# Weaving each layernorm's chunks into the residual loop that feeds it

## The reference, cut to what matters

```python
def _layernorm(x, eps=1e-5):
    m = jnp.mean(x, axis=-1, keepdims=True)
    v = jnp.var(x, axis=-1, keepdims=True)
    return (x - m) / jnp.sqrt(v + eps)

x = x + attn_a(_layernorm(x), ...)   # q, k, v; circular binding of k and v summed over
                                     # the tokens; unbinding of the sum with q
x = x + ffn(_layernorm(x), ...)      # 8 experts of rank 16, the best 2 by gate logits
x = x + attn_b(_layernorm(x), ...)   # layernorms its input again; 16 heads, sigmoid scores
x = x + ffn(_layernorm(x), ...)
```

## Time and profile before

| | us |
|---|---|
| runs of the kernel | 2741.25, 2744.46, 2745.48 (median 2744.46) |
| the profiled execution, its time | 2747.32 |
| its span on the slowest core (core 3) | 2745.8 |
| spans of the 8 cores | 2723.5 to 2745.8 |
| PE busy / DVE / ACT in the span | 1518.3 / 1105.6 / 678.2 |
| mean granted TensorE clock | 0.707 to 0.709 of full speed |

### The profile page before, as it was taken

One profiled execution on the slowest core, in us unless ns is written; L12 is line 12 of the kernel. 1 busy time (PEld: TensorE's weight loads), 2 busy tenths in 40 slices (PEclk: granted clock), 3 DMA queues, 4 the chain that ended last, 5 costly groups with the idle time before them and its releaser, 6 DMA issues.

```text
span 2745.8 us, 19739 instructions; the slowest of 8 cores (2723.5 to 2745.8 us)
## 1 busy us (share of the span) xinstructions
PE 1518.3 (55%) x5930; PEld 574.3 (21%) x5930; DVE 1105.6 (40%) x1281; ACT 678.2 (25%) x677; POOL 36.2 (1%) x58
## 2 busy tenths in 40 slices
PE   1699956131111535448223887878767778775131
PEld 1234422120000212223000222222212222222110
DVE  5422231452366565544996322231132232212631
ACT  0000000000000000000212677776056777650000
POOL 1000000100000000000000000000000000001000
PEclk9999988555555667679555777777867777777555
DMA  7110125814311113120100000000300000006224
GB/s 153 31 31 24 46 69 169 161 54 145 130 61 62 46 46 77 61 44 14 20 0 0 0 1 1 0 1 1 107 16 1 1 0 1 0 8 154 92 85 161
DMA packets 63802, 142.36 MB, mean 52 GB/s; under 512 B 23507, under 2 KB 25043, under 8 KB 63702
## 3 DMA queue, kind: packets, MB, share of 16 engines
q1 hardware_dynamic: 36870, 124.28, 13.9%
q0 software_dynamic: 26832, 16.82, 4.7%
HBM read 119.10 MB, written 37.75 MB: 57 GB/s over the span
## 4 chain that ended last, share of the span: by engine, by line
PE 42%; DVE 19%; DMA 14%; ACT 10%; issue 8%; DVEq 6%; SPq 1%; ACTq 0%; POOLq 0%
DMA xcb<-xb 9%; ACT fmA L1698 8%; PE pP L1724 7%; PE pP L1602 7%; DMA xcb<-x 4%; PE pA L588 3%; PE pP L324 3%; PE pB L588 3%; PE pA L1210 3%; PE pA L1684 3%; PE pP L1684 2%; PE pB L1684 2%; PE pB L1210 2%; DVE xcb L651 2%; DVE h L1379 2%
## 5 line engine op out<-in xcount | busy, mean ns | idle before, releaser
L324 PE MATMUL pP<-ident,scb 128*128 128x128 bf16 x768 | 97.1, 306 | 586.8 <-DVE scb L396 265.8
L1698 ACT ACTIVATE fmA<-pA,cpool 128x1024 bf16<-128x1024 f32 x172 | 209.0, 1215 | 92.6 <-PE pA L1684 92.5
L1698 ACT ACTIVATE fmA<-pP,cpool 128x1024 bf16<-128x1024 f32 x170 | 206.6, 1215 | 91.2 <-PE pP L1684 91.2
L1698 ACT ACTIVATE fmA<-pB,cpool 128x1024 bf16<-128x1024 f32 x170 | 206.6, 1215 | 86.0 <-PE pB L1684 80.9
L324 PEld LDWEIGHTS pP<-ident,scb 128*128 128x128 bf16 x768 | 74.3, 138 | 612.1 <-issue 612.1
L1602 PE MATMUL pP<-fmA,h 128*64 128x512 bf16 x512 | 185.2, 542 | 8.1 <-ACT fmA L1698 7.3
L1724 PE MATMUL pP<-fmA,h 128*64 128x512 bf16 x512 | 186.9, 545 | 4.6 <-ACT fmA L1698 2.8
L1735 DVE COPY h<-pP 64x1024 f32<-64x1024 f32 x32 | 39.1, 1222 | 358.2 <-PE pP L1724 358.2
L1684 PE MATMUL pA<-h 64*128 64x512 bf16 x344 | 121.4, 438 | 52.8 <-ACT fmA L1698 46.3
L1684 PE MATMUL pB<-h 64*128 64x512 bf16 x340 | 120.5, 440 | 50.6 <-ACT fmA L1698 44.1
L1684 PE MATMUL pP<-h 64*128 64x512 bf16 x340 | 119.6, 437 | 51.1 <-ACT fmA L1698 44.6
(11 more groups left out here) (204 smaller groups left out, 1964.8 us busy)
## 6 DMA issues: line engine op xcount, KB each, us to landing
xcb<-xb SPq DMA_DIRECT2D x128, 512.0 KB, 4.0
xb<-xcb SPq DMA_DIRECT2D x48, 512.0 KB, 2.9
xcb<-x SPq DMA_DIRECT2D x32, 512.0 KB, 4.2
y<-xcb SPq DMA_DIRECT2D x16, 512.0 KB, 2.9
skew<-h SPq DMA_DIRECT2D x16, 256.0 KB, 2.5
Wb<-aWk POOLq DMA_DIRECT2D x1, 2048.0 KB, 22.8
h<-aWv POOLq DMA_DIRECT2D x1, 2048.0 KB, 39.7
Wb<-aWq POOLq DMA_DIRECT2D x1, 2048.0 KB, 17.1
```

The costliest lines, as they stand in the source:

```text
L324: mmi = t.transpose(pTb[:, base + 128 * j:base + 128 * (j + 1)], src_bf[:, 128 * j:128 * (j + 1)], ident[:])
L1698: c.inc(s.activation(RB[:, 1024 * sc:1024 * (sc + 1)], ps[:], AF.Sigmoid, bias=cpool[:, 0:1], scale=cpool[:, 1:2]), "S", mark=m_sg)
```

## The change

`ln_fused` gets a lazy form: it makes all its marks at once and hands out `emit`, which appends the next chunk's pieces to the engines' lists, and `flush`, which appends the rest. `resid_out` gets a `hook`, called at the end of each chunk. The layernorms "ba", "c2" and "da" are made ahead of the residual loop that writes their input, and their chunks are appended one by one: chunk t of "ba" behind chunk t of "a8", chunk t of "c2" behind chunk t of "bo". For "da" the hook runs in the second half of "c10" alone: its chunks 0 to 7 are appended behind the chunks 8 to 15 of "c10", and its chunks 8 to 15 after the loop. Each layernorm chunk does what it did; its load still waits for the store of its chunk. The first copy of the gate logits into `xcb` now waits for the last two stores of the loop ahead. The first layernorm, "a2", is built in one go as before.

```diff
     def ln_fused(tag, src, mvbuf, invbuf, dst_fm, fm_guard, src_marks=None,
-                 inner=False):
+                 inner=False, lazy=False):
+        ld_m = [mk(tag + "L") for _ in range(TC)]
...
+        ev_list = [m[1] for m in tp_m]
         lg = ln_guard["m"]
-        for tc in range(TC):
...
+        ln_guard["m"] = ap_m[TC - 1]
+        g0 = last["scb1g"]
+        nctr = [0]
+
+        def emit_chunk():
+            tc = nctr[0]
+            nctr[0] += 1
+            lm, m_st, m_qq, ma = ld_m[tc], st_m[tc], qq_m[tc], ap_m[tc]
+            prev_mm = tp_m[tc - 1][0] if tc else None
 
             @op("y")
-            def _(y, tc=tc, lm=lm, lg=lg):
+            def _(y, tc=tc, lm=lm):
                 if src_marks is not None:
                     c.wait(y, src_marks[tc])
                 if tc >= 2:
-                    c.wait(y, ap_marks[tc - 2])
+                    c.wait(y, ap_m[tc - 2])
...
+            fg = fm_guard["m"] if isinstance(fm_guard, dict) else fm_guard
+            transposes(tag, tc, ma, scb1, dst_fm,
+                       fg if tc == 0 else None, marks=tp_m[tc])
+            last["scb1g"] = tp_m[tc][0]
+
+        def flush():
+            while nctr[0] < TC:
+                emit_chunk()
+
+        obj = {"ev": ev_list, "i2": i2_m, "emit": emit_chunk,
+               "flush": flush}
+        if not lazy:
+            flush()
...
@@ resid_out, at the end of each chunk
+            if hook is not None:
+                hook()
...
+    a8_stm = [mk("a8W") for _ in range(TC)]
+    lnB = ln_fused("ba", dxb0, mv1, inv1, fmA, qev[15], src_marks=a8_stm,
+                   lazy=True)
     a8_ev, a8_st = resid_out("a8", DC, a8_mms, dram["x"], dxb0, "dB",
                              first_wait=(qev[15], "a6Q"),
                              tapname="t_xa" if dbg else None,
-                             load_guard=qev[15])
+                             load_guard=qev[15], stm=a8_stm,
+                             hook=lnB["emit"])
+    lnB["flush"]()
...
@@ ffn_phase
-        m_fm = ln_fused(tag + "a", src, mv1, inv1, fmA, fm_guard,
-                        src_marks=prev_store)
+        if lnobj is None:
+            m_fm = ln_fused(tag + "a", src, mv1, inv1, fmA, fm_guard,
+                            src_marks=prev_store)
+        else:
+            m_fm = lnobj["ev"]
...
                 if tc == 0:
                     c.wait(v, "setup:g")
+                    for m in (prev_store[-2:] if prev_store else ()):
+                        c.wait(v, m)
...
+    b_stm = [mk("boW") for _ in range(TC)]
+    lnC_guard = {"m": None}
+    lnC = ln_fused("c2", dxb1, mv1, inv1, fmA, lnC_guard, src_marks=b_stm,
+                   inner=True, lazy=True)
     mB_st, mB_fmlast = ffn_phase("b", dxb0, dxb1, "t_xb" if dbg else None,
                                  "dB", list(a8_st), qev[15], "w:aWv",
-                                 prev_tap=dbg)
+                                 prev_tap=dbg, lnobj=lnB, out_stm=b_stm,
+                                 out_hook=lnC["emit"],
+                                 out_ln_guard=lnC_guard)
+    lnC["flush"]()
...
@@ after the attention heads
+        if th == 1:
+            last["scb1g"] = qn_prev["ss"]
+            tp_ping["prev"] = [d_chain[0], d_chain[0]]
+            lnD_box[0] = ln_fused("da", dxb0, mv1, inv1, fmA,
+                                  att_done[-1], src_marks=c10_stm,
+                                  lazy=True)
...
+            if th == 1:
+                lnD_box[0]["emit"]()
...
+    lnD = lnD_box[0]
+    lnD["flush"]()
     mD_st, _ = ffn_phase("d", dxb0, dy, None, "dO", list(c10_st),
-                         att_done[-1], "w:bWo", prev_tap=dbg)
+                         att_done[-1], "w:bWo", prev_tap=dbg, lnobj=lnD)
```

More of the change, by code:

```diff
@@ L309, in transposes @@
             toff = 128 * tc
-        m_mm, m_ev = mk(tag + "TM"), mk(tag + "TE")
+        if marks is None:
+            marks = (mk(tag + "TM"), mk(tag + "TE"))
+        m_mm, m_ev = marks
         half = tp_ping["i"] % 2
@@ L340, in ln_fused @@
     def ln_fused(tag, src, mvbuf, invbuf, dst_fm, fm_guard, src_marks=None,
-                 inner=False):
[L342 to L345, removed]
-        lg = ln_guard["m"]
-        for tc in range(TC):
-            lm, m_st, m_qq, ma = (mk(tag + "L"), mk(tag + "S"),
-                                  mk(tag + "Q"), mk(tag + "A"))
-            ap_marks.append(ma)
+                 inner=False, lazy=False):
+        ld_m = [mk(tag + "L") for _ in range(TC)]
+        st_m = [mk(tag + "S") for _ in range(TC)]
+        qq_m = [mk(tag + "Q") for _ in range(TC)]
+        ap_m = [mk(tag + "A") for _ in range(TC)]
+        tp_m = [(mk(tag + "TM"), mk(tag + "TE")) for _ in range(TC)]
+        s2_m = [mk(tag + "T") for _ in range(TC)] if inner else []
+        q2_m = [mk(tag + "U") for _ in range(TC)] if inner else []
+        i2_m = [mk(tag + "I") for _ in range(TC)] if inner else []
+        ev_list = [m[1] for m in tp_m]
+        lg = ln_guard["m"]
+        ln_guard["m"] = ap_m[TC - 1]
[6 more added lines that the diff above has]
+            prev_mm = tp_m[tc - 1][0] if tc else None
             @op("y")
-            def _(y, tc=tc, lm=lm, lg=lg):
+            def _(y, tc=tc, lm=lm):
                 if src_marks is not None:
@@ L387, in _ @@
                 def _(v, tc=tc, m_qq=m_qq, ma=ma, prev_mm=prev_mm,
-                      g0=(last["scb1g"] if tc == 0 else None)):
+                      g0=(g0 if tc == 0 else None)):
                     c.wait(v, m_qq)
@@ L401, in ln_fused @@
             else:
-                m_s2, m_q2, m_i2 = (mk(tag + "T"), mk(tag + "U"),
-                                    mk(tag + "I"))
-                i2_marks.append(m_i2)
+                m_s2, m_q2, m_i2 = s2_m[tc], q2_m[tc], i2_m[tc]
                 @op("v")
                 def _(v, tc=tc, m_qq=m_qq, m_s2=m_s2,
-                      g0=(last["scb1g"] if tc == 0 else None)):
+                      g0=(g0 if tc == 0 else None)):
                     c.wait(v, m_qq)
@@ L446, in _ @@
                     c.inc(v.tensor_copy(scb1[:], scf1[:]), "V", mark=ma)
[L448 to L453, removed]
+            fg = fm_guard["m"] if isinstance(fm_guard, dict) else fm_guard
[9 more added lines that the diff above has]
+            flush()
         if inner:
-            return ev_list, i2_marks
-        return ev_list
+            return obj if lazy else (ev_list, i2_m)
+        return obj if lazy else ev_list
     def ln_pass(tag, src, mvbuf, invbuf, statsmark, dst_fm, fm_guard,
@@ L611, in resid_out @@
     def resid_out(tag, nk, emit_mms, resid_src, resid_dst, store_sem,
-                  first_wait=(), tapname=None, load_guard=None):
-        ev, stm = [], []
+                  first_wait=(), tapname=None, load_guard=None, stm=None,
+                  hook=None):
+        ev = []
+        if stm is None:
+            stm = [mk(tag + "W") for _ in range(TC)]
         for tc in range(TC):
             ps, pn = pick(tc)
-            m_mm, m_ld, m_ev, m_st = (mk(tag + "M"), mk(tag + "R"),
-                                      mk(tag + "E"), mk(tag + "W"))
+            m_mm, m_ld, m_ev = (mk(tag + "M"), mk(tag + "R"),
+                                mk(tag + "E"))
+            m_st = stm[tc]
             pfree = last[pn]
@@ L935, in _ @@
                     c.wait(v, "setup:g")
+                    for m in (prev_store[-2:] if prev_store else ()):
+                        c.wait(v, m)
+                        if prev_tap:
+                            c.wait(v, m + "t")
                 c.inc(v.tensor_copy(gl[:, NE * tc:NE * (tc + 1)],
@@ L1113, in ffn_phase @@
             oguard += [m + "t" for m in prev_store[-2:]]
+        if out_ln_guard is not None:
+            out_ln_guard["m"] = hw_ev[1]
         o_ev, o_st = resid_out(tag + "o", 1, o_mms, src, dst, store_sem,
                                first_wait=(hw_ev[1], tag + "w:fB"),
-                               tapname=tapname, load_guard=tuple(oguard))
+                               tapname=tapname, load_guard=tuple(oguard),
+                               stm=out_stm, hook=out_hook)
         sfree(tag + "cwx")
@@ L1572, in _emit @@
     c10_st = []
+    c10_stm = [mk("cAW") for _ in range(TC)]
+    lnD_box = [None]
     wo_guard = [None]
```

14 lines of the change are left out of this document (6 added, 8 removed).

## The result

The kernel before took 2742.94 us in the median of its runs beside the changed one (2741.25 to 2749.41), the changed kernel 2915.48: +172.5 us. The ratio is 1.0638 (95% interval 1.0613 to 1.0663), 6.4% slower; it is that of the means, without the executions in which the cores of a die ran slowed. The forecast was 2935, its range 2875 to 2980. The profiled execution of the changed kernel took 2915.84, with a span of 2914.3 on its slowest core (core 6), 168.5 more than the 2745.8 of before.

The account below looks back on a forecast made before the run. No engine bounds the kernel; chunks are loops of waits, which the change puts in series. B +108, C +44 and D +39, weight loads at nothing, make +191 on 2744.5: 2935 us, range 2875 to 2980.

Parts of the forecast that it names:

- B: The a8 chunks with layernorm "ba": serial rounds of 19.42 us, 304.1 in place of 195.8, +108 us.
- C: The "bo" chunks with layernorm "c2": serial rounds of 18.05 us, 288.1 against 244.3, +44 us.
- D: Second half of the c10 chunks with "da": rounds of 17.3 us, 177.3 against 138.7, +39 us.
- Rival 4: Store and layernorm load in B and C take their lone latencies, 2.9 and 3.81: 35 us less, 2900; chance 0.2.
- Rival 1: TensorE fast in the bursts of B and D, 3.61 for 5.6: 44 us less, 2891; chance 0.12.
- Rival 3: Weight loads come out from cover at the gates or first "bo" load: +10 us, 2945; chance 0.13.
- Rival 2: Halves overlap in B (-90), C (-77) and D (-39): 2539 us; chance 0.03 with any other gain.

Follow-up runs that it names:

- e4: Changed kernel, but the layernorm "ba" reads the input x instead of the stored chunk, so its load waits for no store; 1.0521, 2886 us.
- e5: Changed kernel, but the layernorm of chunk t-1 is appended behind chunk t, one chunk of lag; 1.0367, 2844 us.
- e9: Changed kernel plus 48 filler matmuls on PE behind each a8 chunk's 16; 1.0535, 2890 us.
- e7: Changed kernel with layernorm loads lagging one chunk, its rest two, and the next chunk's matmuls and residual load put ahead; 0.9284, 2547 us.
- e1: Changed kernel with only "ba" woven, into a8; "c2" and "da" built in one go; 1.0423, 2859 us.
- e3: Changed kernel with only "da" woven, into the second half of c10; "ba" and "c2" built in one go; 1.0168, 2789 us.
- e10: Changed kernel, but POOL's bWq load and the two behind it wait until h is scaled; one profiled execution, 2953.62 us.
- e8: Changed kernel with nothing woven, but the residual load of chunk t+1 ahead of store t; 0.9889, 2712 us.

## Why the prediction was right

**The loop.** The step that carried the forecast, that chunk t+1 stands behind the transposes of chunk t, and those behind a store and the load that reads it back, is shown by the timeline of B and by the experiments from both sides: one chunk of lag with the matmuls ahead brought the time back to that of before, with no instruction of the chunks taken away.

**The terms of a round in B**, forecast and mean measured: add to store issue 1.35 and 1.38; store to the load behind it 3.5 and 3.01; load to statistics 4.3 and 3.97; statistics to transposes 3.68 and 3.70; transposes to matmuls 0.81 and 0.81; matmuls and the way to the add 5.78 and 5.61. The sum is 19.42 against 18.48. Three terms were a little too dear, together 1.0; over 15 rounds and the last chunk that is the 15 us by which B, at 289, fell short of 304. The mechanism was right and these sizes off, half of it the store. In the mean of the eight cores the three were 2.85, 4.02 and 5.36, the round 18.09. B, C and D were all forecast too dear, by 28 together; the 5 us of the gates and of all else, put at nothing, hid a part of that, which is luck.

**Rival 4**, both latencies the lone ones, leant the right way: 3.01 and 3.97 lie near its 2.9 and 3.81, and its 2900 missed 2915.5 by a little less than the forecast's 2935. The landings in the trace of the changed kernel, stores and layernorm loads, against the earlier trace rows:

```profile
DMA to landing us min/median/max: 2.6/2.9/3.1
...
DMA to landing us min/median/max: 3.4/3.9/9.9
```

The long ends, 4.8 and 15.1 before, are shorter, in loops that move 86 GB/s in place of 156 and 124. The 9.9 is a load of the first layernorm, not of these three. Where a load did run beside a store it was slower: 4.73 in e4, 4.53 in e5, 4.85 in D. The page "DMA: Bandwidth & Descriptors" of the Trainium skill, section "Latency and other measured facts", says that the fixed cost falls with a less loaded HBM. These rows agree in direction; that it is HBM and not the queues that tells is not shown by them.

**C and D** came 10 and 3 us below their forecasts. C's round was 17.57 for 18.05, by its store wait (3.10 for 3.5); D's 17.05 for 17.3. D has no wait for a store of its loop and paid only for the exposed load, as forecast.

**Rival 1** did not come: PE waits 12 us ahead of each burst and the bursts took 4.6 to 6.2, mean 5.43, where the mean of three slow ones had been taken, 5.6. What the clock costs in B is shown by e9, 23 us in the mean of the cores, where rival 1 has 15 x 2.0 = 30; the clock in B was 0.65, a little above the 0.5 to 0.6 forecast.

**Rival 3, the weight loads at the gates**, was in part what happened, and the step that costed them at nothing failed by 4.3 us (3.0 in the mean of the cores). Its own mechanism did not come: no instruction waits for those loads, and the first "bo" add did not come late after its load (3.95 idle for it against 4.03 in the earlier trace rows), since bWq landed 20.9 after its issue, at 709.4, and not 29.8, and the first "bo" load goes out at 721.4. What the runs show in its place is a stop on PE without a semaphore while POOL's loads are under way, over each time 1.2 to 1.6 us after a 16 KB instruction transfer has ended; when bWq and the two loads behind it went, the stop fell to 0 to 0.48.

**Rival 2, the interleaving works**, failed in this change for the reason given, and the weaving with two lags came within 8, 1 and 5 us of its prices for B, C and D. The page "Perfetto Trace Analysis" of the Trainium skill, section "Optimization Strategy", says that interleaving stretches with different most-contended engines may improve performance. The changed kernel is against it at +6.4%, e7 for it at -7.2%. The section does not ask for work of another chunk in the gap, as the prediction has it; by these runs the rule does need the condition that what is appended between belongs to a chunk whose inputs are already there.

Still open: why single cores had a lower clock ahead of B in the profiled executions of e1, e3 and e10, which is where the 19 and the 10 above the sums are seen; why the bursts of e4 are slower; and what holds up the instruction transfer.

## What to carry to other kernels

When two loops are merged on in-order queues, write down for one round each queue's order and follow from add to add what must end first: interleaving at the same index puts both loops' latencies in series, at an index one or two back it hides them. The price of the bad case is the plain sum of distances between rows of the old trace, and a good deal of it is a DMA's round trip and TensorE's low clock, not work. Before a weaving is given up as slower, try a lag for each of its steps: the consumer's load by one, its computation by two, and the producer's matmuls ahead.

## What the runs showed of the hardware

- A group of small matmuls stopped for 1.1 to 4.2 us without any semaphore on 8 of 8 cores, while POOL's loads, among them one of 2 MB, were in flight, and for 0 to 0.48 with three of these loads put later. In all 63 such stops of nine kernels PE went on 1.2 to 1.6 us after a 16 KB transfer on the instruction queue had ended.
- A store issued just behind a load on SP's queue lands late. In e7's "do" loop SP issues the residual load 0.47 ahead of the store, and the load after it (2462.78) can go only when that store has landed, 5.72 after its issue:

```profile
2456.59 0.32 SPq L687 DMA_DIRECT2D xcb<-xb  x1
2457.06 0.34 SPq L714 DMA_DIRECT2D y<-xcb  x1
2461.50 1.23 DVE L708 TENSOR_TENSOR xcb<-pA,xcb 128x1024 f32<-128x1024 f32 x1 [6.37 <-DMA xcb<-xb]
2462.78 0.32 SPq L687 DMA_DIRECT2D xcb<-xb  x1
```

```profile
y<-xcb SPq DMA_DIRECT2D x16, 512.0 KB, 5.4
```

  The median from issue to landing is 5.4 for these stores, 2.9 for the changed kernel's, which have no load just ahead of them. The same order stands in e8, with its 4.98. That is why loads ahead bought "do" 0.2 us a round (0.3 in the mean of the eight cores) and not 1.8.
- Sixteen matmuls that take 3.61 at 2.4 GHz took 4.6 to 6.2 when PE had idled some 12 us ahead of the transposes just before them, and the window's mean clock was 0.65.
